# Cross-attention and expert layer on one core: scores computed in 64-row halves of the TensorE array, with the block-diagonal keys built once for all sequences

## The reference

```
x = x + attention(layernorm(x), ctx, ctx)       # softmax over 64 keys, 16 heads of 8
h = layernorm(x)
e = argmax(mean over tokens(h) @ Wr + br)       # one expert for a whole sequence
x = x + relu(h @ W1[e] + b1[e]) @ W2[e] + b2[e]
```

## Time and profile before

| what | value |
|---|---|
| time, median of 3 runs (lowest, highest) | 189.23 us (189.15, 191.22) |
| profiled execution: span from first to last instruction | 186.4 us |
| PE, DVE, ACT, POOL busy | 163.8, 130.8, 103.7, 102.8 us |
| granted TensorE clock, mean | 1.000 |

### The profile page before, as it was taken

One profiled execution on the slowest core, in us unless ns is written; L12 is line 12 of the kernel. 1 busy time (PEld: TensorE's weight loads), 2 busy tenths in 40 slices (PEclk: granted clock), 3 DMA queues, 4 the chain that ended last, 5 costly groups with the idle time before them and its releaser, 6 DMA issues.

```text
span 186.4 us, 4892 instructions
## 1 busy us (share of the span) xinstructions
PE 163.8 (88%) x1414; PEld 128.7 (69%) x1414; DVE 130.8 (70%) x380; ACT 103.7 (56%) x261; POOL 102.8 (55%) x215
## 2 busy tenths in 40 slices
PE   0427787789999999989999999999999999999893
PEld 0215673545786969686969696969696969687583
DVE  1165877789696888878696969696968686857300
ACT  3333355456666658573939393939393927264240
POOL 0405845384856674677584958585858555232220
PEclk9999999999999999999999999999999999999999
DMA  6994188143445453635171727171717272431540
GB/s 177 328 329 120 43 170 203 39 100 111 116 114 143 113 146 70 189 101 147 33 220 32 218 43 215 41 209 32 225 31 230 54 201 65 111 108 54 155 155 28
DMA packets 20751, 24.33 MB, mean 131 GB/s; under 512 B 2304, under 2 KB 16128, under 8 KB 20736
## 3 DMA queue, kind: packets, MB, share of 16 engines
q1 hardware_dynamic: 18896, 22.85, 45.5%
q10 hardware_dynamic: 1840, 1.30, 2.4%
HBM read 13.13 MB, written 2.10 MB: 82 GB/s over the span
## 4 chain that ended last, share of the span: by engine, by line
PE 69%; issue 8%; POOL 5%; ACT 5%; DMA 4%; DVE 4%; SPq 2%; POOLq 0%; ACTq 0%; DVEq 0%
PE ps_pv L564 15%; PE ps_ring L553 13%; PE ps_max L524 8%; PE ps_ring L542 8%; PE ps_q L578 7%; PE ps_pv L578 6%; POOL k_diag L332 4%; DMA x_sb<-in_x 3%; PE ps_o L678 3%; PE ps_o L632 3%; PE ps_q L598 3%; SPq L279 2%; PE ps_max L638 2%; ACT probs_t L412 2%; DVE negmax L732 1%
## 5 line engine op out<-in xcount | busy, mean ns | idle before, releaser
L732 DVE TENSOR_REDUCE negmax<-ps_max 128x8 f32<-128x512 f32 x64 | 41.7, 675 | 4.8 <-PE ps_max L524 4.5
L332 POOL TENSOR_TENSOR k_diag<-k_stack,cst 96x256 fp32r<-96x256 f32 x64 | 37.6, 617 | 7.9 <-DMA k_stack<-k_parts 6.2
L412 ACT ACTIVATE probs_t<-ps_ring 128x512 f32<-128x512 f32 x64 | 34.6, 595 | 9.7 <-PE ps_ring L542 9.7
L564 PE MATMUL ps_pv<-ew,hid_t 128*128 128x128 f32 x256 | 33.7, 276 | 0.5 <-ACT hid_t L419 0.5
L553 PE MATMUL ps_ring<-xn_t,ew 128*128 128x256 f32 x128 | 33.8, 392 | 0.1
L564 PEld LDWEIGHTS ps_pv<-ew,hid_t 128*128 128x128 f32 x256 | 31.2, 191 | 1.5 <-issue 1.2
L419 ACT ACTIVATE hid_t<-ps_ring,ew 128x256 f32<-128x256 f32 x64 | 25.5, 480 | 9.7 <-PE ps_ring L553 9.7
L319 POOL TENSOR_TENSOR ve<-mv,eps_sb 128x2 f32<-128x2 f32 x32 | 6.3, 196 | 42.2 <-DVE mv L746 36.1
L783 DVE RECIPROCAL inv_sum<-ps_q 128x256 f32<-128x256 f32 x16 | 28.0, 1750 | 1.8 <-PE ps_q L578 1.8
L542 PE MATMUL ps_ring<-q_stack,k_diag 112*128 112x256 f32 x128 | 26.9, 317 | 0.1
L524 PE MATMUL ps_max<-k_diag,q_stack 96*128 96x256 f32 x128 | 23.2, 302 | 3.8 <-POOL k_diag L332 2.1
(11 more groups left out here) (62 smaller groups left out, 218.8 us busy)
## 6 DMA issues: line engine op xcount, KB each, us to landing
q_stack<-q_parts SPq DMA_DIRECT2D x64, 96.0 KB, 2.3
ew<-in_experts SPq DMA_DIRECT2D x16, 320.0 KB, 3.1
ew<-in_experts SPq DMA_DIRECT2D x16, 258.0 KB, 2.7
out_y<-y_sb SPq DMA_DIRECT2D x16, 128.0 KB, 1.8
x_sb<-in_x SPq DMA_DIRECT2D x2, 768.0 KB, 10.8
k_stack<-k_parts SPq DMA_DIRECT2D x4, 288.0 KB, 4.6
q_stack<-negmax_t SPq DMA_DIRECT2D x16, 64.0 KB, 2.4
ctx_sb<-in_ctx_t ACTq DMA_DIRECT2D x1, 768.0 KB, 11.4
```

Source lines behind the costliest of these rows:

```text
L332: nc.gpsimd.tensor_tensor(k_diag[0:SR, par, g * GK:(g + 1) * GK].rearrange("r (h k) -> r h k", h=HG), k_stack[:, g, bass.ds(n * KEYS, KEYS ...
L412: nc.scalar.activation(probs_t[:, 2 * g:2 * g + 2, :], ps_ring[(2 + g) % 3][:], ACT.Exp, scale=SCALE).then_inc(exp_done, 1)
L564: mm = nc.tensor.matmul(ps_pv[:, 0, q * P:(q + 1) * P], hid_t[:, c, q * P:(q + 1) * P], w2_of(par, c), start=(c == 0 and q == 0), stop=(c ...
L732: nc.vector.tensor_reduce(negmax[:, par, q, half * 8:(half + 1) * 8], ps_max[half][:].rearrange("p (h k) -> p h k", k=KEYS), AX_X, ALU.max ...
```

## The change

The scores are computed in the upper and the lower 64 rows of the array, each half with its own matmul. A half and a slot hold two heads of 32 rows each: a feature takes four consecutive rows, of which one holds the high query against the high key, one the low query against the high key, one the high query against the low key, and one is free; in one of the free rows the maximum of the head stands. `q_stack` is now 128 rows by 4 slots, zeroed once and filled by three DMAs a sequence that write every fourth row.

The maximum is taken over scores of the rounded high parts alone: `scores_for_max` multiplies `q_parts` (no longer `q_stack`) with a new `k_all`, in which each of eight copies of the high keys keeps the rows of one head of a half. DVE builds it once (`place_k`, 8 instructions for the first four sequences, 8 for the other twelve). Two matmuls of 64 rows by 512 columns stand for four of 96 rows by 256.

`k_diag` now holds all sequences; POOL builds it in four large instructions (`diag_k`), from a `k_stack` that POOL zeroes at the start. The four small instructions for each sequence are gone, as are DVE's two copies of the ones (L711), the copies of high parts (L699 on DVE, L435 on ACT) and the loop: all 23 steps are written out with constant indices. `scores_t` writes slots 0 and 1 of both halves in one part and slots 2 and 3 in the other; the second part follows all of `down`.

```diff
-        k_diag = sb("k_diag", [P, 2, GROUPS * GK], F32R)
+        k_all = sb("k_all", [P, 2 * SLOTS, B * KEYS], F32R)
+        k_diag = sb("k_diag", [P, SLOTS, B, 2, KEYS], F32R)
...
+        SCORE_BANK = [ps_ring[0], ps_ring[1], ps_ring[2], ps_ring[0]]
+        UP_BANK = [ps_ring[1], ps_ring[2]]
...
-                for g in range(GROUPS):
-                    sp.dma_start(k_stack[:, g, cols], k_parts[GR * g:GR * (g + 1), :, cols].bitcast(F32)
-                                 ).then_inc(landed, 16)
+                for row, part in enumerate((0, 0, 1)):
+                    sp.dma_start(k_stack[row::4, :, cols], k_parts[:, part, cols].bitcast(F32)
+                                 ).then_inc(kstack_in[group], 16)
...
-                    for g in range(GROUPS):
-                        sp.dma_start(q_stack[0:SR, par, g, :].bitcast(F32),
-                                     q_parts[GR * g:GR * (g + 1), par].bitcast(F32)).then_inc(qstack_in[par], 16)
+                for row in (0, 2):
+                    sp.dma_start(q_stack[row::4, par].bitcast(F32), q_parts[:, par, 0, :].bitcast(F32)
+                                 ).then_inc(qstack_in[par], 16)
+                sp.wait_ge(qlo_done, n + 1)
+                sp.dma_start(q_stack[1::4, par].bitcast(F32), q_parts[:, par, 1, :].bitcast(F32)
+                             ).then_inc(qstack_in[par], 16)
...
+            for cols in K_GROUPS:
+                nc.gpsimd.memset(k_stack[:, :, cols], 0.0).then_inc(kzero_done, 1)
...
+            def diag_k(group, h):
+                batches = B_GROUPS[group]
+                pool.wait_ge(kstack_in[group], 16 * 3)
+                nc.gpsimd.tensor_scalar(k_diag[:, :, batches, h, :],
+                                        k_stack[:, :, K_GROUPS[group]].rearrange("p s (b k) -> p s b k", k=KEYS),
+                                        const_col("half_mask", h), const_col("max_rows", h), ALU.mult, ALU.add
+                                        ).then_inc(kdiag_done, 1)
...
+            def scores_for_max(n, q):
+                par = n % 2
+                if q == 0:
+                    pe.wait_ge(qhi_done, n + 1)
+                    pe.wait_ge(kall_done, group_of(n) + 1)
+                    if n >= 1:
+                        pe.wait_ge(max_done, 4 * n)
+                        pe.wait_ge(maxt_done, n)
+                else:
+                    pe.wait_ge(max_done, 4 * n + 2)
+                for i in range(2):
+                    rows = slice(HALF * i, HALF * (i + 1))
+                    nc.tensor.matmul(ps_max[i][:], q_parts[rows, par, 0, q * P:(q + 1) * P],
+                                     k_all[rows, :, n * KEYS:(n + 1) * KEYS], start=True, stop=True
+                                     ).then_inc(smax_done, 1)
...
+                for low in range(2):
+                    for i in range(2):
+                        rows = slice(HALF * i, HALF * (i + 1))
+                        slot = 2 * part + low
+                        mm = nc.tensor.matmul(SCORE_BANK[2 * part + i][:, low, :],
+                                              k_diag[rows, slot, n].rearrange("p h k -> p (h k)"),
+                                              q_stack[rows, par, slot, :], start=True, stop=True)
+                        if low == 1:
+                            mm.then_inc(s_done, 1)
...
+            nc.vector.memset(q_stack[:].bitcast(F32), 0.0).then_inc(qzero_done, 1)
...
+            def place_k(group, heads):
+                cols = K_GROUPS[group]
+                for m in heads:
+                    st = nc.vector.tensor_scalar(k_all[:, m, cols], k_parts[:, 0, cols].bitcast(F32),
+                                                 const_col("head_mask", m), None, ALU.mult)
...
+                if t == 0:
+                    place_k(1, range(4))
+                if t == 1:
+                    place_k(1, range(4, 8))
```

More of the change, by code:

```diff
@@ L221, in xattn_moe_kernel, with live, group_of @@
         rstd2_done = sem("rstd2_done")
[L223 to L244, removed]
+        STEPS = range(-3, B + 4)
+        def live(n):
+            return 0 <= n < B
+        def group_of(n):
+            return 0 if n < FIRST_B else 1
         block = ctx.enter_context(nc.Block())
@@ new lines, in max_transposed, with normalise1 @@
+            def max_transposed(n):
+                par = n % 2
+                act.wait_ge(tmax_done, n + 1)
+                if n >= 2:
+                    act.wait_ge(max_in[par], 16 * (n // 2))
+                nc.scalar.copy(negmax_t[:, par, :], ps_max[1][0:HEADS, 0:TOK]).then_inc(maxt_done, 1)
+            def normalise1(n):
+                par = n % 2
+                act.wait_ge(shift1_done, n + 1)
+                if n >= 2:
+                    act.wait_ge(tr1_done, n - 1)
+                for q in range(QT):
+                    nc.scalar.activation(xn1[:, par, q, :], x_sb[:, n, q, :], ACT.Identity,
+                                         scale=rstd1[:, par, q, :], bias=shift1[:, par, q, :]
+                                         ).then_inc(xn1_done, 1)
@@ L547, in up @@
-            def up(i, j, half, exp_before):
-                n, par = 2 * i + j, j % 2
+                if quarter == 2:
+                    pe.wait_ge(klo_done, 1)
+                if quarter == 3:
+                    pe.wait_ge(klo_done, 3)
+                bank = V_BANKS[quarter].rearrange("p a t -> p (a t)")
+                for k in range(4):
+                    mm = nc.tensor.matmul(bank[:, k * D:(k + 1) * D], ctx_sb[:, 4 * quarter + k, :],
+                                          const("wv_t"), start=True, stop=True)
@@ L555, in up, with down @@
                 mm.then_inc(up_done, 1)
-            def down(i, j, half):
-                n, par = 2 * i + j, j % 2
+            def down(n, half):
+                par = n % 2
                 pe.wait_ge(hid_done, 4 * n + 2 * half + 2)
@@ new lines, in _ @@
+            for t in STEPS:
+                if live(t):
+                    scores_for_max(t, 0)
+                if live(t - 1):
+                    scores_t(t - 1, 0)
+                if live(t + 1):
+                    project_q(t + 1)
+                if t == 0:
+                    project_k([1, 2])
+                    project_v(0)
+                    project_v(1)
+                if live(t - 4):
+                    n = t - 4
+                    pe.wait_ge(down_in[n % 2], 16 * (n // 2 + 1))
+                    if live(t - 2):
@@ L838, in step @@
                     st.then_inc(st2_raw, 1)
-            pipeline(dve, step, {-3: lambda: dve.wait_ge(x_in[1], 16), -2: first_k, -1: rest, 0: later,
-                                 4: lambda: dve.wait_ge(x_in[3], 16)})
+                if t == -2:
+                    dve.wait_ge(cst_in[0], 16)
+                    dve.wait_ge(cst_in[1], 16)
+                    low_k([0])
+                    dve.wait_ge(khi_done, 1)
+                    place_k(0, range(8))
+                if t == 0:
+                    place_k(1, range(4))
+                if t == 1:
+                    place_k(1, range(4, 8))
 _ARGS = ["x", "ctx_t", "consts", "experts"]
```

729 lines of the change are left out of this document (335 added, 394 removed).

## The result

The changed kernel takes 197.95 us (median of 4 runs, 197.72 to 199.94); the kernel before, run beside it, 189.75 (189.15 to 191.22). The ratio is 1.0471, 95% interval 1.0421 to 1.0522: slower. A ratio here compares only those runs of both kernels that lie within 1.5% of the fastest of their kernel, so it need not be the quotient of the two medians. The profiled execution spans 196.0 us, 9.6 more than before.

The account below looks back on a forecast made before the run. PE, busy 88%, was taken to bound the kernel, a step being PE alone. From 189.2 us, start -1.8, eleven steps +2.9 and end +1.0 gave 191.3 us; own range 188 to 193, with rivals 183.5 to 198.

Parts of the forecast that it names:

- -1.8 us at step 4: Start: step 1 4.0 us earlier (21.2), key copies +3.5, shorter waits, so step 4 begins 1.8 us earlier, near 49.
- The eight `place_k`: Steps 1 to 3: DVE's eight copies of 768 elements, 0.5 us each, add 4.0, 0.5 of it hidden: +3.5 us.
- The step: Steady step on PE: -0.63 for matmuls, +0.30 for changes, +0.70 for the wait; 9.69 us instead of 9.32.
- The transposed scores: Each step on PE: eight matmuls in four pairs, 0.20 a pair because of weight loads, 0.80 us.
- The three changes of division: Each step on PE: three more changes between ways of dividing the array, 0.10 each, 0.30 us; bounds 0 and 0.45.
- The pairs for the maximum: Each step on PE: two pairs of 512-column matmuls, halves running at once, 0.24 a pair, 0.48 us.
- the wait: Each step: the sum's second half waits on PE for ACT's exponentials of groups 2 and 3, adding 0.7 us (0.6 to 0.8).
- The end: After step 15: two more steps with the wait of 0.7 and fewer matmuls to save on, +1.0 us.
- the halves in turn: Rival: matmuls of two halves run one after the other, nothing is saved, a step is 10.32; 199.7 us, chance 0.14.
- Full overlap with free changes: Rival: pairs at 0.24 and 0.12, dividing the array costs nothing, a step is 9.07; 183.5 us, chance 0.20.
- the drains: Rival: every change costs 0.15, no same-half load overlaps a matmul, a step is 9.88; 193.8 us, chance 0.10.
- The dear keys: Rival: large `place_k` take 1.0 each, or POOL's slow instructions hold up the norms; about 195, both 198; chance 0.15.

Follow-up runs that it names:

- both cures: Changed kernel with the eight 768-element key copies on GpSimd with two operations, and the second half of `down` in front of the sum: 185.23 us, ratio 0.9841.
- the run with fewer fillers: Changed kernel plus 4, 6 and 2 unread matmuls on PE before the second scores for the maximum in steps 1, 2, 3: 194.97 us, ratio 1.0327.
- the run with the parts apart: Changed kernel with the second half of `down` moved behind the second transposed scores and second scores for the maximum, before the sum: 191.61 us, ratio 1.0181.
- the early matmuls: As both cures, plus 3 and 4 unread matmuls before the first and second transposes of the normed tokens: 185.33 us, ratio 0.9722.
- the second such run: As the early matmuls, with GpSimd's eight key copies split, four in step 0 and four at the end of step 1: 183.24 us, ratio 0.9675.
- the run with both in one half: Changed kernel with all matmuls over 64 rows in the upper half, same number, size and order of instructions, output wrong: 209.1 us, ratio 1.1059.

## Why the prediction was wrong

The step that failed is "-1.8 us at step 4"; it measured +6.0. What it had wrong above all is PE's rate: the start was laid out with PE's durations at the full clock, and PE at half rate was a term put at nothing. The parts of the miss, from the profiled executions:

- The eight `place_k`: 0.54 us a copy, and +3.5 was predicted for all. From step 1 to step 4 it takes 28.55 us with the copies on DVE and 24.67 with the copies off it (48.83 - 24.16, both cures), both at a full clock; the copies thus cost 3.9. This term held but for 0.4, by luck: the row of 0.28 us for 256 elements gives 0.84 for 768 by proportion, not the 0.5 that I took from it, and eight of those would be 6.7.
- PE's clock: not in the sum at all, +4.1 in this execution. I had the waits for the maxima as lost time only; what runs behind them also ran at 1.2 GHz. The run with fewer fillers shows it alone: the copies stay on DVE, the clock is full, and the 4.1 us are gone. The size is that of one execution, since the same first steps cost 1.5 in the run with the parts apart.
- Step 1: predicted 21.2, came at 24.15, +2.95. Of this 1.23 lies before the first scores, at 13.43 for 12.2: the low part of the keys began at 9.72 for 9.41, the eight copies of 256 elements took 2.18 for some 1.7, and from 12.85 PE has two transposes in front of the scores that the layout left out. The other 1.7 lies between the first scores and step 1, 10.72 us for 9.0. There PE's rows are longer than later ones (0.79 for 0.50), though the granted clock reads 1.00 up to 24 us in this trace; that PE was at half rate is read from the durations alone. With the early matmuls the same way took 9.43 us (13.05 to 22.48), in the second such run more. How much the rate accounts for stays open.
- Steps 1 to 3 without the clock's part: 28.55 for 27.8 (49.0 - 21.2), +0.75; in it is the 0.4 of the copies.

Together 4.1 + 2.95 + 0.75 = 7.8, the distance from -1.8 to +6.0. The start of the kernel before varies too: step 4 began at 50.81 there and at 52.48 with the loop written out.

**The step** came out at 9.75 for 9.69, but by two errors that cancel. The transposed scores, predicted at 0.80, cost 0.48: their loads add nothing that can be seen. The three changes of division, predicted at 0.30, cost 0.20 each, 0.60. The pairs for the maximum were right (0.46 for 0.48), and the wait nearly so (0.77 for 0.70). The sum is -1.91 + 0.46 + 0.48 + 0.60 + 0.77 = +0.40, of the 0.43 measured. The bound of 0.45 for three changes, from two rows, was too low; the 0.22 on entering quarters was no guide to entering halves. The Trainium skill (TensorEngine Tiling (Array Packing), section Key Properties) says that a change of tiling mode drains the array; a price of 0.20 in either direction agrees with it, though no row shows the drain itself. The Trainium skill (TensorE: Matmul & The Clock Gate, section Part 3: Packing small matmuls) also has loads overlap running matmuls only of other row groups. The run with both in one half disagrees: 0.47 for four matmuls of one half, where this rule would give 0.84.

The wait is more than half of what it and the changes of division cost together (0.77 of 1.37). The run with the parts apart shows this: without the wait a step takes 9.27, a little below the 9.32 of before. It misses the expected 9.18 by 0.09; the pair that follows the transposed scores without a change takes 0.37 there, not 0.23, and why is open.

**The end** came out at +0.3 for a predicted +1.0; why it is less was not tried. DVE took nothing over: it waits 1.49 us for the output projection in a step, before 1.39.

Of the rivals, the halves in turn are refuted by the run with both in one half. Full overlap with free changes had the pairs right and the changes wrong; the drains had the changes nearly right (0.15 for 0.20) and the loads wrong. The dear keys gave the right size of time (195 to 198) by the wrong mechanism, since a copy cost 0.54 and PE waited for POOL nowhere in the changed kernel.

## What to carry to other kernels

A piece of one-off work put in front of something that TensorE waits for costs more than its own length where TensorE's clock falls behind the wait: here 3.9 us of copies brought 4.1 us of half-rate work in one execution and 1.5 in another. Price a new way to divide the array by its changes, 0.20 us each here, and keep all work of one division together. If a result needs another engine before the next instruction can run, put work that needs nothing in between: half of `down` was worth 0.48 us a step.

## What was not expected of the hardware

- PE's clock fell behind waits of 1.78, 2.23, 3.30 and 9.22 us; behind the last the granted clock was 0.50, which is 1.2 GHz, from 35 to 46 us. No length of wait separates a fall from none here: in step 3, waits of 1.2 and 0.60 us stood in front of a fall in the changed kernel (product 1.76) and of none in the run with the parts apart (1.07), whose instructions are the same up to there.
- GpSimd's copy of 768 elements by a mask column took 2.18 us with one operation and 0.96 with two, the same bytes and the same output. DVE's, with one, took 0.54.
